# A two-layer transformer tower on one core: the out-projection moved to the end of its slot, its residual and norm to the next slot, and the transposes of h1 ahead of the embedding

## The chip, the core and the metric

The kernel runs on one core of a Trainium2 chip. Its engines each take their own instructions in program order: TensorE (PE, with its weight loads shown apart as PEld), VectorE (DVE), ScalarE (ACT), GpSimd (POOL) and SyncE (SP, which here only issues DMAs). They wait for each other through semaphores. The metric is the device time of one execution in microseconds. Every kernel is timed in several runs, and one execution is also profiled.

## What is computed

64 images of 3 x 112 x 112 are cut into 49 patches of 16 x 16 each, which makes 3136 tokens of 192 values. Then, with every value in float32:

```
h   = patches @ W.T                                  # embedding, 768 -> 192
h1  = layernorm(h  + attention1(h))                  # 12 heads of 16, causal, with relative positions
out = layernorm(h1 + attention2(h1))                 # qkv = h1 @ Wqkv.T + bqkv + delta
# delta: softmax router over 8 experts, the best 2 kept, a low-rank product of rank 16 each
# attention2 has no mask; layernorm(x) = (x - mean) / sqrt(var + 1e-5), without scale or shift
```

Attention works inside one image of 49 tokens. Both attentions end in an out-projection, a matmul of the attended values (192) with a 192 x 192 matrix and a bias.

## The kernel before

The work has two grains. **Tiles** are 2 images, 98 tokens (32 of them); attention proper works on tiles. **Blocks** are 128 tokens (25 of them, b = 0 to 24, the last with 64); every product over tokens works on blocks. A tile and a layer together make one **slot**: slots 0 to 7 are layer 1 of tiles 0 to 7, then layers 2 and 1 alternate (even slots layer 2, odd slots layer 1) until layer 1 is done in slot 55; slots 56 to 63 are layer 2. Each engine has its own list, written as one loop over the slots n, and runs it in order. The lists are the same on each run, and no planner moves instructions beyond what follows.

In slot n PE computes the scores of that slot's tile (L466 adds the causal mask in layer 1, L472 is q times k). It transposes the probabilities of the slot before (L497) and weights the values with them (L508). DVE takes the row maxima of the scores (L763), subtracts them (L770), waits for ACT's exponential (L653), sums (L775), inverts (L780) and scales (L784). That last step releases L497 of the next slot. ACT copies PSUM to SBUF: the transposed probabilities `pt` (L667), the weighted values `yt` (L672).

The products over blocks are spread over the slots. For a block b, in this order of slots:

- `embed` (L414, 6 steps, each matmul issued as two) writes bank 5, ACT's `take_h` (L627) copies it to h.
- `turns`: `transpose_h` (L426, L427, bank 6), then q, k, v of layer 1 (`project_v` L484 in bank 6, `project_qk1` L436 and L438 in bank 4). ACT's `take_qk` copies k (L644) and then q (L646) out of bank 4 and raises `qk_ready`.
- `out1`: two slots after its last tile, `out_project` (L519, L520) writes bank 5. DVE adds the residual (`add_residual`, L791) and takes the statistics (`ln_stats` L797, `ln_aggregate` L803). ACT takes a logarithm and an exponential (`inverse_deviation`, L699 and L702). POOL computes a shift (L385) and h1 = res * rstd + shift (L388).
- `turns1`: the slot after `out1`. `transpose_h1` (L530) writes bank 4, ACT's `take_h1` (L680) copies it, and at the end of the same slot `route` (L540, L542) computes the router's input in bank 7.
- `routers`: the slot after that, DVE's `router_max` and `combine` (L808 to L829), then PE's `transpose_hw` (L548, L549).
- `qkv2s`: `project_v` (L484) and `project_qk2` (L449, L451, L453, bank 4) for layer 2.
- `out2`: as `out1` for layer 2, and SP stores the block.

EMBED, QKV1 and QKV2, the tables that say which slot a block's products fall into, come from a small balancing loop at the head of the file; it is the same in both kernels.

Two variables carry PSUM's bank rules: `bank4` and `bank5` hold the semaphore that the next user of the bank must wait for. After `project_qk` the next user of bank 4 waits for `qk_ready`; after `transpose_h1` it waits for `h1t_ready`. After `embed` the next user of bank 5 waits for `h_ready`; after `out_project`, for `res_ready`. `transpose_probs` waits for `yt_ready` of the weighting before it, since both use bank 2.

Below are the functions that the change touches.

Of the kernel before, what the change touches and what calls it, by code (L numbers as in the profile page):

```python
# [71 lines left out]
SLOT1 = [CHAINS.index((1, t)) for t in range(TILES)]  # L72
# [10 lines left out]
DONE1 = [SLOT1[last_tile(b)] + (b == BLOCKS - 1) for b in range(BLOCKS)]  # L83
DONE2 = [SLOT2[last_tile(b)] + (b == BLOCKS - 1) for b in range(BLOCKS)]
FIRST = -3
SLOTS = max(DONE2) + 3


WORK = {n: 0.0 for n in range(-9, SLOTS)}
# [82 lines left out]
def build(nc, x, tok_w, w1a_in, w1b_in, pos_in, const_in, p1_in, lora_in, w2_in, b2_in, p2_in, out):  # L172
    with ExitStack() as ctx:
# [132 lines left out]
        @block.sync  # L306
        def _(sp):
            def load_x(b):
                sp.dma_start(xs[:, b % XS], x[b]).then_inc(x_loaded[b % XS], 16)

            for u in range(3):
                sp.dma_start(xs[:, 0, 2 * u:2 * u + 2], x[0, :, 2 * u:2 * u + 2]).then_inc(x0_loaded[u], 16)
            load_x(1)
            sp.dma_start(w1a[:], w1a_in).then_inc(w1a_loaded, 16)
            sp.dma_start(w1b[:], w1b_in).then_inc(w1b_loaded, 16)
            sp.dma_start(tail[64:128, 0:POS], pos_in[:, 0:POS]).then_inc(pos_loaded[0], 16)
            load_x(2)
            load_x(3)
            sp.dma_start(p1[:], p1_in).then_inc(p1_loaded, 16)
            sp.dma_start(tail[64:128, POS:TOK], pos_in[:, POS:TOK]).then_inc(pos_loaded[1], 16)  # L320
            sp.dma_start(lora[:], lora_in).then_inc(lora_loaded, 16)
            load_x(4)
            sp.dma_start(w2[:], w2_in).then_inc(w2_loaded, 16)
            sp.dma_start(b2[:], b2_in).then_inc(b2_loaded, 16)
            sp.dma_start(p2[:], p2_in).then_inc(p2_loaded, 16)

            def place_values(L, t, slot_of):
                sp.wait_ge(L.v_rows, block_of(t) + 1)
                if t >= VB:
                    sp.wait_ge(pv_done, slot_of[t - VB] + 1)  # L330
                for b, row, s, at, k in moves(t):
                    for e in range(2):
                        sp.dma_start(L.vbd[t % VB][e * PB + at:e * PB + at + k, s].rearrange("p (u e c) -> p u e c", u=3, e=2)[:, :, e],
                                     L.vrow[b % VR][row:row + k, e * C:(e + 1) * C].rearrange("p (u c) -> p u c", u=3)).then_inc(L.v_ready[t % VB], 16)

            sp.wait_ge(zeros_ready, 2)
            for n in range(FIRST, SLOTS):
                for b in embeds(n):
                    if b + XS < BLOCKS:
                        sp.wait_ge(emb_done, b + 1)  # L340
                        load_x(b + XS)
                for t in tiles_from(n - 1, QKV1):
                    place_values(L1, t, SLOT1)
                for t in tiles_from(n - 1, QKV2):
                    place_values(L2, t, SLOT2)
                for b in out2(n):
                    k = tokens(b)
                    sp.wait_ge(L2.ln_ready, b + 1)
                    sp.dma_start(out[first_token(b):first_token(b) + k], o_sb[b % OS][0:k]
                                 ).then_inc(out_stored[b % OS], 16)  # L350
            for u in range(OS):
                sp.wait_ge(out_stored[u], 16 * len(range(u, BLOCKS, OS)))

        @block.gpsimd
        def _(pool):
# [35 lines left out]
            block_diagonal(0)  # L391
            block_diagonal(1)
            for n in range(SLOTS):
                for b in out1(n):
                    normalise(L1, b, h[0:tokens(b), b, :])
                for b in out2(n):
                    if b >= OS:
                        pool.wait_ge(out_stored[b % OS], 16 * (b // OS))
                    normalise(L2, b, o_sb[b % OS][0:tokens(b)])
                block_diagonal(n + 2)  # L400

        @block.tensor
        def _(pe):
# [158 lines left out]

            for n in range(FIRST, SLOTS):
                layer, t = attention(n)
                before, u = attention(n - 1)
                if layer == 1:
                    scores(L1, t, n)
                if layer == 2:
                    scores(L2, t, n)
                for b in out1(n):  # L570
                    if b == 0:
                        pe.wait_ge(p1_loaded, 16)
                        pe.wait_ge(ones_ready, 1)
                    bank5 = out_project(L1, p1, b, SLOT1, bank5)
                for b in out2(n):
                    if b == 0:
                        pe.wait_ge(p2_loaded, 16)
                    bank5 = out_project(L2, p2, b, SLOT2, bank5)
                for b in turns(n):
                    bank6 = transpose_h(b, bank6)  # L580
                if before:
                    if n == 1:
                        pe.wait_ge(zeros_ready, 2)
                    transpose_probs(n - 1)
                for b in turns1(n):
                    bank4 = transpose_h1(b, bank4)
                for b in qkv2s(n):
                    pe.wait_ge(hwt_ready, b + 1)
                    if b == 0:
                        pe.wait_ge(w2_loaded, 16)  # L590
                        pe.wait_ge(b2_loaded, 16)
                    bank6 = project_v(L2, b, values2(b), bank6)
                    bank4 = project_qk2(b, bank4)
                for b in turns(n):
                    pe.wait_ge(ht_ready, b + 1)
                    if b == 0:
                        pe.wait_ge(w1a_loaded, 16)
                        pe.wait_ge(w1b_loaded, 16)
                        pe.wait_ge(pos_loaded[0], 16)
                    if first_token(b) + tokens(b) > POS >= first_token(b):  # L600
                        pe.wait_ge(pos_loaded[1], 16)
                    bank6 = project_v(L1, b, values1(b), bank6)
                    bank4 = project_qk1(b, bank4)
                for b in embeds(n):
                    bank5 = embed(b, bank5)
                if before == 1:
                    weigh_values(L1, u, n - 1)
                if before == 2:
                    weigh_values(L2, u, n - 1)
                for b in routers(n):  # L610
                    transpose_hw(b)
                for b in turns1(n):
                    if b == 0:
                        pe.wait_ge(lora_loaded, 16)
                    route(b)

        @block.scalar
        def _(act):
# [85 lines left out]

            for n in range(FIRST, SLOTS):
                layer, t = attention(n)
                before, u = attention(n - 1)
                for b in routers(n):
                    router_exp(b)
                for b in turns(n):  # L710
                    take_ht(b)
                if before:
                    take_pt(n - 1)
                for b in turns1(n):
                    take_h1(b)
                if n == 0:
                    act.wait_ge(masks_ready, 1)
                if layer:
                    exponent(n)
                for b in qkv2s(n):  # L720
                    take_v(L2, b, SLOT2)
                    take_qk(L2, b, SLOT2)
                for b in out1(n):
                    inverse_deviation(L1, b)
                for b in out2(n):
                    inverse_deviation(L2, b)
                for b in turns(n):
                    take_v(L1, b, SLOT1)
                    take_qk(L1, b, SLOT1)
                for b in embeds(n):  # L730
                    take_h(b)
                if before:
                    take_y(n - 1, u)
                for b in routers(n):
                    take_hw(b)

        @block.vector
        def _(dve):
# [94 lines left out]

            for n in range(SLOTS):
                layer, t = attention(n)
                for b in routers(n):
                    router_max(b)
                if layer:
                    largest(n)
                    subtract(n)  # L840
                for b in out1(n):
                    add_residual(L1, b)
                for b in out2(n):
                    add_residual(L2, b)
                for b in out1(n):
                    ln_stats(L1, b)
                for b in out2(n):
                    ln_stats(L2, b)
                for b in routers(n):
                    combine(b)  # L850
                for b in out1(n):
                    ln_aggregate(L1, b)
                for b in out2(n):
                    ln_aggregate(L2, b)
                if layer:
                    sum_probs(n)
                    invert_sums(n)
# [80 lines left out]
```

## Time and profile before

| what | value |
|---|---|
| median of 3 runs | 447.51 us (447.36 to 451.51) |
| the profiled execution, whole | 446.53 us |
| its span, first to last instruction | 444.7 us |
| mean granted clock of TensorE | 0.958 of full |
| PE, PEld, DVE, ACT, POOL busy | 398.6, 348.5, 295.0, 231.7, 116.6 us |

The profiled execution is 0.98 us below the median. The span lacks 1.8 us that lie around it. In the profile a row of the timeline gives the start in microseconds from the span's start, the busy time, the engine, the source line, the operation, what it writes and reads, and in brackets how long the engine stood idle before it and for whom it waited. Ends of matmuls are modelled and overlap the start of the next, so PE's pace is read from start to start.

The slots can be told apart in the timeline by the start of L472. Slot 13 begins at 119.35, slot 14 at 124.83, slot 15 at 129.24, slot 24 at 185.10 and slot 25 at 192.56.

### The profile page before, as it was taken

How to read it: one execution, taken by the hardware profiler on the slowest of the kernel's cores; microseconds unless marked ns; L12 is line 12 of the kernel's file. 1: busy time of each engine (PE TensorE's matmuls, PEld its weight loads, DVE VectorE, ACT ScalarE, POOL GpSimd, SP SyncE). 2: the span in 40 equal slices, each digit the busy share in tenths (PEclk: the TensorE clock that was granted, in tenths of full speed). 3: DMA queues.
4: the chain of work that ended last, by engine and by line, in shares of the span. 5: the costliest groups of instructions: out<-in, count | busy, mean ns of one | idle time of the engine just before them, and what ended most of it. 6: DMA issues, size and time to landing. Idle time of an engine off the chain costs nothing.

```text
span 444.7 us, 13552 instructions
## 1 busy us (share of the span) xinstructions
PE 398.6 (90%) x5270; PEld 348.5 (78%) x5270; DVE 295.0 (66%) x783; ACT 231.7 (52%) x727; POOL 116.6 (26%) x237
## 2 busy tenths in 40 slices
PE   5874997999989999999999999989998999887974
PEld 4763886878878898889888899778886988776853
DVE  7051566857677676876687767696578758777572
ACT  1341455465565656555665555646655565544442
POOL 1110112230233213432242222333223223313122
PEclk9995999999999999999999999999999999996875
DMA  8452221210212111220221212111101110111010
GB/s 282 131 159 63 50 80 18 51 38 15 48 28 62 50 48 28 64 54 11 50 64 25 57 45 58 28 19 30 18 19 19 30 18 19 17 23 22 14 32 23
DMA packets 49353, 21.23 MB, mean 48 GB/s; under 512 B 41278, under 2 KB 45601, under 8 KB 49226
## 3 DMA queue, kind: packets, MB, share of 16 engines
q1 hardware_dynamic: 48714, 19.64, 18.1%
q8 instruction: 42, 0.69, 0.6%
q10 hardware_dynamic: 576, 0.73, 0.5%
q14 instruction: 21, 0.17, 0.1%
HBM read 13.13 MB, written 2.41 MB: 35 GB/s over the span
## 4 chain that ended last, share of the span: by engine, by line
PE 73%; ACT 9%; DVE 8%; issue 5%; DMA 3%; SPq 1%; POOLq 0%; POOL 0%; ACTq 0%; DVEq 0%
PE ps L414 11%; PE ps L484 10%; PE ps L497 8%; PE ps L472 7%; PE ps L519 5%; PE ps L508 5%; PE ps L449 4%; PE ps L453 4%; PE ps L451 4%; PE ps L436 3%; PE ps L438 3%; PE ps L520 3%; DVE mx L763 2%; PE ps L540 2%; ACT q L646 2%
## 5 line engine op out<-in xcount | busy, mean ns | idle before, releaser
L763 DVE TENSOR_REDUCE mx<-ps 113x12 f32<-113x588 f32 x64 | 49.2, 769 | 75.4 <-PE ps L472 74.8
L378 POOL TENSOR_SCALAR kbd<-k,const 64x294 f32<-64x294 f32 x128 | 69.1, 549 | 98.1 <-ACT q L646 88.0
L667 ACT COPY pt<-ps 113x339 f32<-113x339 f32 x128 | 50.7, 445 | 52.1 <-PE ps L497 51.7
L385 POOL TENSOR_SCALAR shift<-mv,rstd 128x1 f32<-128x1 f32 (+1 forms) x50 | 13.2, 264 | 216.4 <-ACT rstd L702 216.4
L414 PE MATMUL ps<-tokw,xs 128*128 128x192 f32 (+1 forms) x300 | 57.1, 342 | 9.1 <-DVE res L791 4.8
L775 DVE TENSOR_REDUCE psum<-probs 113x12 f32<-113x588 f32 x64 | 48.4, 756 | 23.7 <-ACT probs L653 22.9
L414 PEld LDWEIGHTS ps<-tokw,xs 128*128 128x128 f32 (+1 forms) x300 | 50.7, 197 | 11.4 <-DVE res L791 6.4
L497 PE MATMUL ps<-const,probs 113*113 113x113 f32 x384 | 52.1, 274 | 3.4 <-DVE probs L784 2.6
L784 DVE TENSOR_TENSOR probs<-probs,rsum 113x588 f32<-113x588 f32 x64 | 51.4, 802 | 2.2
L497 PEld LDWEIGHTS ps<-const,probs 113*113 113x113 f32 x384 | 47.2, 186 | 6.6 <-issue 5.1
L770 DVE TENSOR_TENSOR probs<-ps,mx 113x588 f32<-113x588 f32 x64 | 49.4, 772 | 2.2
L644 ACT COPY k<-ps 64x384 f32<-64x384 f32 (+11 forms) x60 | 24.0, 417 | 51.4 <-PE ps L453 40.6
L472 PE MATMUL ps<-kbd,q 32*49 32x98 f32 x1536 | 47.5, 252 | 0.0
L653 ACT ACTIVATE probs<-probs 113x588 f32<-113x588 f32 x64 | 45.6, 713 | 2.4 <-DVE probs L770 1.2
L508 PE MATMUL ps<-pt,vbd 113*32 113x49 f32 x1536 | 36.8, 214 | 10.9 <-DMA vbd<-vrow 9.6
L508 PEld LDWEIGHTS ps<-pt,vbd 113*32 113x32 f32 x1536 | 27.9, 112 | 21.7 <-DMA vbd<-vrow 9.8
L472 PEld LDWEIGHTS ps<-kbd,q 32*49 32x49 f32 x1536 | 34.0, 120 | 9.0 <-issue 3.8
L519 PE MATMUL ps<-p,yt 96*128 96x192 f32 (+1 forms) x100 | 30.7, 390 | 8.3 <-ACT yt L672 6.7
L449 PE MATMUL ps<-h1t,w 96*128 96x128 f32 (+1 forms) x150 | 29.4, 277 | 0.0
L436 PE MATMUL ps<-ht,w1a 128*128 128x128 f32 (+1 forms) x150 | 29.3, 276 | 0.0
L451 PE MATMUL ps<-h1t,w 105*128 105x128 f32 (+1 forms) x150 | 29.2, 276 | 0.0
L453 PE MATMUL ps<-hwt,b 128*128 128x128 f32 (+1 forms) x150 | 29.2, 276 | 0.0
(79 smaller groups left out, 704.2 us busy)
## 6 DMA issues: line engine op xcount, KB each, us to landing
xs<-in_x SPq DMA_DIRECT2D x24, 384.0 KB, 3.7
vbd<-vrow SPq DMA_DIRECT2D x160, 18.4 KB
out<-o SPq DMA_DIRECT2D x24, 96.0 KB, 1.7
tail<-in_pos SPq DMA_DIRECT2D x1, 656.0 KB, 16.2
tokw<-in_tokw ACTq DMA_DIRECT2D x3, 192.0 KB, 3.4
w<-in_w SPq DMA_DIRECT2D x1, 472.5 KB, 10.0
xs<-in_x SPq DMA_DIRECT2D x3, 128.0 KB, 3.2
p<-in_p SPq DMA_DIRECT2D x2, 145.5 KB
```

Source lines behind the costliest of these rows:

```text
L378: last = nc.gpsimd.tensor_scalar(L.kbd[t % 2][:, e], L.k[:, :, at:at + T], kmask[:, e:e + 1], 1.0, ALU.mult, ALU.mult)
L414: last = nc.tensor.matmul(ps[0:k, 5, 0:E], xs[:, b % XS, m, 0:k], tokw[:, m, :], start=(m == 0), stop=(m == KX - 1))
L449: nc.tensor.matmul(ps[:, 4, m * NB:m * NB + k], w2[0:C, 1, cols], h1t[0:C, 1, b % HB2, 0:k], start=True, stop=False)
L472: last = nc.tensor.matmul(ps[s * PB:s * PB + S, half, m * T:(m + 1) * T], L.q[32 * half:32 * half + 32, m, at + s * S:at + (s + 1) * S], L ...
L497: last = nc.tensor.transpose(ps[0:PP, 2 + half, g * PP:(g + 1) * PP], pf[:, k:k + PP], ident[0:PP, 0:PP])
L508: last = nc.tensor.matmul(ps[32 * g:32 * g + 32, 2, half * T + s * S:half * T + (s + 1) * S], values[:, s, (3 * half + g) // 2, :, (3 * ha ...
L519: nc.tensor.matmul(ps[0:k, 5, 0:E], yt[0:C, 1, lo:lo + k], w[0:C, 1, :], start=True, stop=False)
L667: nc.scalar.copy(pt[n % 2][:, 3 * half:3 * half + 3, :].rearrange("p g i -> p (g i)"), ps[0:PP, 2 + half, 0:3 * PP]).then_inc(pt_ready[hal ...
L763: nc.vector.tensor_reduce(mx[:].rearrange("p (b h) -> p b h", b=2), score_view, AX.X, ALU.max).then_inc(mx_ready, 1)
L770: nc.vector.tensor_tensor(probs_view(n), score_view, spread(mx), ALU.subtract).then_inc(sub_ready, 1)
L775: nc.vector.tensor_reduce(psum[:].rearrange("p (b h) -> p b h", b=2), probs_view(n), AX.X, ALU.add).then_inc(sum_ready, 1)
L784: nc.vector.tensor_tensor(probs_view(n), probs_view(n), spread(rsum), ALU.mult).then_inc(p_ready, 1)
```

## The change

PE's list within a slot was: scores, out-projection, transposes of h, transposes of the probabilities, transposes of h1, q, k, v of layer 2, q, k, v of layer 1, embedding, weighting, the router's parts. It is now: scores, transposes of h, transposes of the probabilities, q, k, v of layer 2 and of layer 1, transposes of h1, embedding, out-projection, weighting, the router's parts. On DVE the residual, the statistics and the aggregate stand at the head of the next slot's list, ahead of the router's maximum and the row maxima. On ACT `inverse_deviation` stands in the next slot between `take_ht` and `take_pt`, and `take_h1` follows the copies of q and k. On POOL the normalisation, and on SP the store of a block, are one slot later. The loops run over one slot more, so that the last block's norm is reached.

```diff
--- before.py
+++ after.py
@@ -83,7 +83,7 @@
 DONE1 = [SLOT1[last_tile(b)] + (b == BLOCKS - 1) for b in range(BLOCKS)]
 DONE2 = [SLOT2[last_tile(b)] + (b == BLOCKS - 1) for b in range(BLOCKS)]
 FIRST = -3
-SLOTS = max(DONE2) + 3
+SLOTS = max(DONE2) + 4
 
 
 WORK = {n: 0.0 for n in range(-9, SLOTS)}
@@ -343,7 +343,7 @@
                     place_values(L1, t, SLOT1)
                 for t in tiles_from(n - 1, QKV2):
                     place_values(L2, t, SLOT2)
-                for b in out2(n):
+                for b in out2(n - 1):
                     k = tokens(b)
                     sp.wait_ge(L2.ln_ready, b + 1)
                     sp.dma_start(out[first_token(b):first_token(b) + k], o_sb[b % OS][0:k]
@@ -391,9 +391,9 @@
             block_diagonal(0)
             block_diagonal(1)
             for n in range(SLOTS):
-                for b in out1(n):
+                for b in out1(n - 1):
                     normalise(L1, b, h[0:tokens(b), b, :])
-                for b in out2(n):
+                for b in out2(n - 1):
                     if b >= OS:
                         pool.wait_ge(out_stored[b % OS], 16 * (b // OS))
                     normalise(L2, b, o_sb[b % OS][0:tokens(b)])
@@ -567,23 +567,12 @@
                     scores(L1, t, n)
                 if layer == 2:
                     scores(L2, t, n)
-                for b in out1(n):
-                    if b == 0:
-                        pe.wait_ge(p1_loaded, 16)
-                        pe.wait_ge(ones_ready, 1)
-                    bank5 = out_project(L1, p1, b, SLOT1, bank5)
-                for b in out2(n):
-                    if b == 0:
-                        pe.wait_ge(p2_loaded, 16)
-                    bank5 = out_project(L2, p2, b, SLOT2, bank5)
                 for b in turns(n):
                     bank6 = transpose_h(b, bank6)
                 if before:
                     if n == 1:
                         pe.wait_ge(zeros_ready, 2)
                     transpose_probs(n - 1)
-                for b in turns1(n):
-                    bank4 = transpose_h1(b, bank4)
                 for b in qkv2s(n):
                     pe.wait_ge(hwt_ready, b + 1)
                     if b == 0:
@@ -601,8 +590,19 @@
                         pe.wait_ge(pos_loaded[1], 16)
                     bank6 = project_v(L1, b, values1(b), bank6)
                     bank4 = project_qk1(b, bank4)
+                for b in turns1(n):
+                    bank4 = transpose_h1(b, bank4)
                 for b in embeds(n):
                     bank5 = embed(b, bank5)
+                for b in out1(n):
+                    if b == 0:
+                        pe.wait_ge(p1_loaded, 16)
+                        pe.wait_ge(ones_ready, 1)
+                    bank5 = out_project(L1, p1, b, SLOT1, bank5)
+                for b in out2(n):
+                    if b == 0:
+                        pe.wait_ge(p2_loaded, 16)
+                    bank5 = out_project(L2, p2, b, SLOT2, bank5)
                 if before == 1:
                     weigh_values(L1, u, n - 1)
                 if before == 2:
@@ -709,10 +709,12 @@
                     router_exp(b)
                 for b in turns(n):
                     take_ht(b)
+                for b in out1(n - 1):
+                    inverse_deviation(L1, b)
+                for b in out2(n - 1):
+                    inverse_deviation(L2, b)
                 if before:
                     take_pt(n - 1)
-                for b in turns1(n):
-                    take_h1(b)
                 if n == 0:
                     act.wait_ge(masks_ready, 1)
                 if layer:
@@ -720,13 +722,11 @@
                 for b in qkv2s(n):
                     take_v(L2, b, SLOT2)
                     take_qk(L2, b, SLOT2)
-                for b in out1(n):
-                    inverse_deviation(L1, b)
-                for b in out2(n):
-                    inverse_deviation(L2, b)
                 for b in turns(n):
                     take_v(L1, b, SLOT1)
                     take_qk(L1, b, SLOT1)
+                for b in turns1(n):
+                    take_h1(b)
                 for b in embeds(n):
                     take_h(b)
                 if before:
@@ -833,25 +833,25 @@
 
             for n in range(SLOTS):
                 layer, t = attention(n)
+                for b in out1(n - 1):
+                    add_residual(L1, b)
+                for b in out2(n - 1):
+                    add_residual(L2, b)
+                for b in out1(n - 1):
+                    ln_stats(L1, b)
+                for b in out2(n - 1):
+                    ln_stats(L2, b)
+                for b in out1(n - 1):
+                    ln_aggregate(L1, b)
+                for b in out2(n - 1):
+                    ln_aggregate(L2, b)
                 for b in routers(n):
                     router_max(b)
                 if layer:
                     largest(n)
                     subtract(n)
-                for b in out1(n):
-                    add_residual(L1, b)
-                for b in out2(n):
-                    add_residual(L2, b)
-                for b in out1(n):
-                    ln_stats(L1, b)
-                for b in out2(n):
-                    ln_stats(L2, b)
                 for b in routers(n):
                     combine(b)
-                for b in out1(n):
-                    ln_aggregate(L1, b)
-                for b in out2(n):
-                    ln_aggregate(L2, b)
                 if layer:
                     sum_probs(n)
                     invert_sums(n)
```

**PE, slot 14** (layer 2 of tile 3, no product of q, k, v in it; `yt_ready` is ACT's copy of the weighted values, `ln_ready1` POOL's norm of layer 1). Before:

```order
L472 MATMUL ps<-kbd_1,q 49x98 x11
L519 MATMUL ps<-p,yt 128x192 [waits yt_ready,res_ready1]
L520 MATMUL ps<-p,yt 128x192
L497 MATMUL ps<-const,probs 113x113 [waits p_ready,yt_ready]
L497 MATMUL ps<-const,probs 113x113 x5
L530 MATMUL ps<-const,h 96x128 [waits ln_ready1,qk_ready1]
L530 MATMUL ps<-const,h 96x128
L508 MATMUL ps<-pt,vbd_2 32x49 [waits pt_ready0,v_ready1_2]
```

and now:

```order
L472 MATMUL ps<-kbd_1,q 49x98 x11
L497 MATMUL ps<-const,probs 113x113 [waits p_ready,yt_ready]
L497 MATMUL ps<-const,probs 113x113 x5
L530 MATMUL ps<-const,h 96x128 [waits ln_ready1,qk_ready1]
L530 MATMUL ps<-const,h 96x128
L519 MATMUL ps<-p,yt 128x192 [waits yt_ready,res_ready1]
L520 MATMUL ps<-p,yt 128x192
L508 MATMUL ps<-pt,vbd_2 32x49 [waits pt_ready0,v_ready1_2]
```

The out-projection went from ahead of the transposes to directly ahead of the weighting, and the norm that `ln_ready1` stands for now starts with DVE's residual in this slot, not in the one before.

**PE, slot 16** (layer 2 of tile 4, with the q, k, v of a block; `qk_ready2` is ACT's copy of q and k out of bank 4, `h1t_ready` its copy of the transposed h1 out of the same bank). Before:

```order
L530 MATMUL ps<-const,h 96x128 [waits ln_ready1,h1t_ready]
L530 MATMUL ps<-const,h 96x128
L484 MATMUL ps<-w,h1t 128x192 [waits v_rows1,hwt_ready]
L484 MATMUL ps<-w,h1t 128x192
L484 MATMUL ps<-b,hwt 128x192
L449 MATMUL ps<-h1t,w 128x128 [waits h1t_ready]
```

and now:

```order
L449 MATMUL ps<-h1t,w 128x128
L451 MATMUL ps<-h1t,w 128x128
L453 MATMUL ps<-hwt,b 128x128
L530 MATMUL ps<-const,h 96x128 [waits ln_ready1,qk_ready2]
L530 MATMUL ps<-const,h 96x128
L519 MATMUL ps<-p,yt 128x192 [waits yt_ready,res_ready1]
```

The two users of bank 4 changed places: three matmuls of another bank (L484) stood between them, and now none does.

**PE, slot 15** (layer 1 of tile 11, with an embedding). Before:

```order
L519 MATMUL ps<-p,yt 128x192 [waits yt_ready,res_ready2]
L520 MATMUL ps<-p,yt 128x192
L497 MATMUL ps<-const,probs 113x113 [waits p_ready,yt_ready]
L497 MATMUL ps<-const,probs 113x113 x5
L414 MATMUL ps<-tokw,xs 128x192 [waits x_loaded0,res_ready1]
L414 MATMUL ps<-tokw,xs 128x192 x5
```

and now:

```order
L497 MATMUL ps<-const,probs 113x113 [waits p_ready,yt_ready]
L497 MATMUL ps<-const,probs 113x113 x5
L414 MATMUL ps<-tokw,xs 128x192 [waits x_loaded0,res_ready2]
L414 MATMUL ps<-tokw,xs 128x192 x5
L519 MATMUL ps<-p,yt 128x192 [waits yt_ready,h_ready]
L520 MATMUL ps<-p,yt 128x192
```

The two users of bank 5 changed places too: the embedding waited for DVE's residual, and now the out-projection waits for ACT's copy of h.

## Rows read from the trace of the kernel before

**Rows 1.** The page: span, busy time, and the chain that ended last.
```profile
span 444.7 us, 13552 instructions
PE 398.6 (90%) x5270; PEld 348.5 (78%) x5270; DVE 295.0 (66%) x783; ACT 231.7 (52%) x727; POOL 116.6 (26%) x237
...
PE 73%; ACT 9%; DVE 8%; issue 5%; DMA 3%; SPq 1%; POOLq 0%; POOL 0%; ACTq 0%; DVEq 0%
```

**Rows 2.** Waits: engine, line, releaser: us in total, times, longest.
```profile
PE ps L519 <- ACT yt L672: 6.7, 16, 0.7
...
PE ps L414 <- DVE res L791: 4.8, 7, 0.9
...
PE ps L540 <- ACT hwt L694: 4.8, 5, 1.5
...
PE ps L508 <- ACT pt L667: 1.0, 5, 0.4
```

**Rows 3.** Timeline, all engines, end of slot 24.
```profile
190.87 0.39 PE L453 MATMUL ps<-hwt,b 128*128 128x128 f32 x2
...
191.19 0.55 PE L508 MATMUL ps<-pt,vbd 113*32 113x49 f32 x24
191.30 0.47 ACT L644 COPY k<-ps 64x384 f32<-64x384 f32 x1 [1.61 <-PE ps L453]
...
191.67 0.50 PE L540 MATMUL ps<-lora,h1t 96*128 96x136 f32 x2
191.78 0.48 ACT L646 ACTIVATE q<-ps 64x384 f32<-64x384 f32 x1
```

**Rows 4.** Timeline, head of slot 24.
```profile
186.11 0.31 ACT L672 COPY yt<-ps 96x196 f32<-96x196 f32 x1
...
186.57 0.56 PE L519 MATMUL ps<-p,yt 96*128 96x192 f32 x2 [0.74 <-ACT yt L672]
...
187.29 0.76 PE L497 MATMUL ps<-const,probs 113*113 113x113 f32 x6
```

**Rows 5.** Timeline of PE, before slot 0: an embedding, then transposes of its h.
```profile
12.35 2.12 PE L414 MATMUL ps<-tokw,xs 128*128 128x192 f32 x12
14.96 0.30 PE L426 MATMUL ps<-const,h 128*128 128x128 f32 x1 [0.50 <-ACT h L627]
```

**Rows 6.** Timelines of DVE, ACT and POOL, slot 31: residual to norm.
```profile
230.87 0.35 DVE L791 TENSOR_TENSOR res<-ps,h 128x192 f32<-128x192 f32 x1
...
231.65 0.18 DVE L803 BATCH_NORM_AGGREGATE mv<-st 128x2 f32<-128x6 f32 x1
...
232.36 0.20 ACT L702 ACTIVATE rstd<-lnv 128x1 f32<-128x1 f32 x1
...
233.02 0.50 POOL L388 TENSOR_SCALAR h<-res,rstd,shift 128x192 f32<-128x192 f32 x1
```

**Rows 7.** Timelines of DVE (first row) and PE, slot 14 and the start of 15.
```profile
124.46 0.89 DVE L784 TENSOR_TENSOR probs<-probs,rsum 113x588 f32<-113x588 f32 x1
...
124.83 0.72 PE L472 MATMUL ps<-kbd,q 32*49 32x98 f32 x24
...
126.63 0.76 PE L497 MATMUL ps<-const,probs 113*113 113x113 f32 x6
127.22 0.38 PE L530 MATMUL ps<-const,h 128*96 128x128 f32 x2
...
129.24 0.72 PE L472 MATMUL ps<-kbd,q 32*49 32x98 f32 x24
```

**Rows 8.** Windows: stretch, its length, busy us of each engine, granted clock, DMA.
```profile
66.00:69.60 3.60, 2.41 (x39) 1.98 (x38) 2.87 (x12) 2.69 (x9) 1.52 (x3) 1.00 0.15 23
...
400.50:404.00 3.50, 2.11 (x52) 1.53 (x43) 2.90 (x10) 2.73 (x11) 3.07 (x8) 1.00 0.10 31
404.00:414.00 10.00, 8.60 (x52) 7.59 (x53) 7.84 (x24) 2.68 (x8) 0.38 (x1) 0.51 0.10 16
...
424.50:428.00 3.50, 2.00 (x55) 1.56 (x53) 2.85 (x8) 1.97 (x6) 1.64 (x4) 1.00 0.16 43
```

## The prediction

> **What bounds the kernel now.** I read the page first, for who is busy: PE 398.6 us of the 444.7 us span, no other engine over 66%, and 73% of the chain that ended last lies on PE [rows 1]. The list of waits then says what PE still waits for: in the body of the program only short things, 6.7 us in 16 waits for `yt` ahead of the out-projection, 4.8 us in 7 waits of the embedding for the residual, 4.8 us in 5 waits of `route` for `hwt`, 1.0 us for `pt` [rows 2]. So PE's list runs nearly without a gap, and the other engines have slack. The third view is the timeline, slot by slot. It gives PE's pace from start to start, and for the change it gives the one thing that matters: how long after PE's last write into a bank the copy out of it is done. A wait that is taken from PE's list is a gain at most as large as these rows, a wait that is put into it is a loss in full, as nothing stands behind PE that could make it up.
>
> **The change, part by part.** It removes no instruction and adds none; every term is a wait on PE that goes or comes. The counts come from the lists of both kernels.
>
> *Transposes of h1 directly after q and k (bank 4).* In 19 slots (4, 5, 6, 8, 9, 10, 16, 18, 24, 26, 28, 32, 34, 36, 42, 44, 50, 52, 58) L530 now follows the last matmul of q and k and must wait until ACT has copied k and then q out of bank 4. In slot 24 the last L453 pair starts at 190.87, the copies begin at 191.30 and end at 192.26, and PE went on with L508 at 191.19 [rows 3]. A copy's end reaches PE 0.15 later: `yt` ends at 186.42, L519 starts at 186.57 [rows 4]. So L530 would start at 192.41 where PE could have gone on at about 191.16: 1.25 us each, **+23.8**. It was hidden before because the order was the other way round: ACT's one copy of h1 was covered by the value matmuls.
>
> *Out-projection directly after the embedding (bank 5).* In 16 slots (3, 4, 7, 9, 15, 17, 22, 25, 27, 30, 33, 35, 41, 43, 49, 51) it waits for `take_h`. The same pair, an embedding and something that needs its copy, stands before slot 0: L414 from 12.35 for 2.12, and the next PE instruction at 14.96, with 0.50 of shown idle and 0.56 against PE's pace [rows 5]. **+9.0**.
>
> *Transposes of h1 in slots without q, k, v.* In slots 14, 22, 40, 48, 56 and 59 nothing stands between the transposes of the probabilities and L530, and the norm now starts with the residual at this slot's head. From the residual's start to the norm's end took 2.65 us in slot 31 (230.87 to 233.52) [rows 6]. PE reaches L530 1.24 after the slot's start: 0.65 for the scores and 0.59 from L497 to L530 [rows 7]. When does the residual start? DVE must first finish the probabilities of the slot before, which it did 0.52 into slot 14 (125.35 against 124.83) [rows 7]. The transposes of the probabilities in slot 13 come 1.1 earlier (0.72 of out-projection [rows 4] and its share of the `yt` waits, 0.4, no longer stand ahead), ACT's logarithm and exponential, now ahead of `pt`, take back 0.5, and the slot itself is 0.4 shorter: 0.3 into the slot. So L530 waits 0.3 + 2.65 - 1.24 = 1.7, of which I take 1.6, as ACT's queue will be shorter than in slot 31, for slots 14, 22, 40 and 48. Slots 56 and 59 follow long slots, in which the residual starts right behind the out-projection, 0.25 before the slot's end: 1.2 each. **+8.8**.
>
> *Behind that.* `route` needs the copy of h1. In the 7 of the 19 slots without an out-projection only the weighting (0.48, L508 to L540 [rows 3]) lies between L530 and `route`; transposing, copying and telling PE take about 0.2 more: **+1.4**. At the end of the program the out-projection of block 22 moves from a gap in PE to between the last transposes and the last weighting: 0.72 of issue, at half clock **+1.4**.
>
> *What goes.* The embedding finds bank 5 free: **-4.8** [rows 2]. The `yt` waits come from ACT being busy with q and k when the weighting ends; the out-projection now stands between them (0.72 longer) and the longest of them was 0.74: **-6.7** [rows 2]. The `pt` waits are covered: **-1.0**. ACT has copied q and k by the time `route` waits for `hwt`, so of 4.8 some **-1.5** goes.
>
> DVE: the residual, statistics and aggregate (0.96 from 230.87 to 231.83 [rows 6]) move from the shadow of the exponential to the slot's head, where DVE otherwise waits for the scores. It costs PE nothing as long as slots are long, which they now are; if that cover is gone the row maxima come late and the next transposes with them, up to 0.4 in some short slots, which I leave to the range. POOL gets its norm earlier in a slot, and its `kbd` work is for two slots later; SP's store stands behind the value DMAs, which have slots to spare. Both: nothing.
>
> Sum: 23.8 + 9.0 + 8.8 + 1.4 + 1.4 - 4.8 - 6.7 - 1.0 - 1.5 = **+30.4**. Against the profiled execution's 446.53 us that is 476.9; the median of the runs is 0.98 higher, so 478.
>
> *The clock.* TensorE's granted clock went from 1.00 to about half (2.4 to 1.2 GHz) at 404, after a stretch of 3.50 us in which PE was busy 2.11, and again after 424.5 to 428.0 with 2.00 of 3.50. It did not after 66.0 to 69.6 with 2.41 of 3.60 [rows 8]. The new waits of 1.6 us in slots 14, 22, 40 and 48, between work of small tiles, make stretches like the first two. One dip costs what PE does in 10 us at half clock: 8.60 busy would have been 4.3 [rows 8], less what its own waits would have taken there, 3.7. I cannot tell whether a given wait sets it off, and bound it by none (0) and by all six short slots (+22). I take one more than before: **+3.7**, nearer the low end, as the new stretches are no emptier than the two that fell and stand among full ones. Forecast: **482**.
>
> **Rivals.**
>
> *The clock falls often.* All six short slots, and some of the 19, whose wait of 1.25 is followed by the weighting and a short wait of `route`, bring the clock down. For it: PE was busy 60% before the clock fell at 404, and the new stretches come near that. Against it: slot 5's wait of 1.5 [rows 2] lies in the stretch that brought no fall. Six dips: 478 + 22 = 500.
>
> *The waits are smaller.* The norm is ready in the short slots (DVE earlier, ACT's queue free), no dip is added, and ACT's copies overlap PE's modelled end more than I read: q and k at 1.0, h at 0.45. 19 x 1.0 + 16 x 0.45 + 3 + 1 - 14 = +16: 463. For it: ends of matmuls are modelled. Against it: the 0.15 is a measured gap.
>
> *Not slower.* The new waits are made up, because PE's list is not what sets the pace: its weight loads fill only 348.5 us [rows 1], and 96 us of the span have none. If PE issues tighter after each wait, only the removed waits count: 446.5 - 14 + 1 = 433.5, or up to 450 with part of it. It decides if the matmuls after a wait start closer together than those without; but L508 follows L453 at the pace of the others, and L519 to L497 took 0.72 behind a wait of 0.74 [rows 4], the pace of work without one, so I hold it unlikely. The Trainium skill (Perfetto Trace Analysis, section Identifying the Most-Contended Engine) says that the matmul busy share is not a good measure of how near a kernel is to its limit and that the share of weight loads is; by it this kernel would have a fifth of its span to give. The same page (Optimizing Tensor Performance, Matmuls) asks that independent groups rotate through banks so that a copy overlaps the next group's matmuls, which the new order gives up in banks 4 and 5; by it the sum stands.
>
> That the change does not do what it says can be left out: the lists show the moves.
>
> **The numbers.** The forecast of 482 (own range 474 to 491) has 0.47, the clock 0.25, smaller waits 0.24, not slower 0.04. The range reaches halfway into both neighbours, 464 to 500, and leaves out less than 2 in 10. A change under 1% could not be told from none: faster by more than that 0.02 and within it 0.02, both from the last rival; slower 0.96.
>
> **What would show it.** In the waits of the changed kernel: L530 for ACT's q, 19 times and near 1.15 us shown; L519 for ACT's h, 16 times near 0.5; L530 for POOL's h, about 6 times, over 1 us; `yt` and residual waits of L519 and L414 nearly gone. PE's idle grows by about 30 us and its busy time only with the clock. The prediction is wrong if L530's waits for q are few or short, or if the time grows far beyond PE's idle at full clock.

## The result, and the profile after

The changed kernel takes 477.62 us (median of 4 runs, 473.4 to 481.71), the kernel before beside it 449.51 us (447.36 to 452.06): ratio 1.059, 95% interval 1.048 to 1.071. The profiled execution took 476.86 us with a span of 475.1 us, 30.4 us more than the span before. The median lies inside the range of 464 to 500 and 4.4 us under the forecast of 482; slower was the forecast. Ratios and intervals, here and below, leave out runs that took over 1.5% longer than the fastest of their kernel.

The page after, against [rows 1]: PE was busy 9 us longer, and idle some 21 us longer. The new waits are shown some 0.2 us shorter than they hold PE up (1.06 against 1.27 below), as they are counted from the modelled end of the matmul before them; that part counts as busy here, beside what the clock costs.

```profile
span 475.1 us, 13552 instructions
PE 407.7 (86%) x5270; PEld 349.3 (74%) x5270; DVE 297.3 (63%) x783; ACT 240.5 (51%) x727; POOL 110.8 (23%) x237
```

The list of waits after, against [rows 2] (us in total, times, longest):

```profile
PE ps L530 <- ACT q L646: 20.6, 19, 1.2
...
PE ps L519 <- ACT h L627: 6.7, 16, 0.6
PE ps L530 <- POOL h L388: 6.2, 6, 1.2
...
PE ps L540 <- ACT hwt L694: 3.3, 5, 0.7
...
PE ps L508 <- ACT pt L667: 1.0, 1, 1.0
...
PE ps L519 <- ACT yt L672: 0.5, 1, 0.5
```

The first three lines are new, with the counts 19, 16 and 6 that the lists of instructions gave. The 16 waits for `yt` are down to one, and the waits of the embedding for the residual are gone.

The end of slot 24 after, all engines, against [rows 3]:

```profile
206.82 0.39 PE L453 MATMUL ps<-hwt,b 128*128 128x128 f32 x2
...
207.25 0.48 ACT L644 COPY k<-ps 64x384 f32<-64x384 f32 x1 [0.97 <-PE ps L453]
207.73 0.48 ACT L646 ACTIVATE q<-ps 64x384 f32<-64x384 f32 x1
...
208.27 0.42 PE L530 MATMUL ps<-const,h 128*96 128x128 f32 x2 [1.06 <-ACT q L646]
```

PE used to start its next work 0.32 us after the start of the last L453 pair; now 1.45 us pass. The shown idle, 1.06, is counted from the modelled end of the matmul.

Slot 27 after (PE; an embedding and the next to need its copy out of the bank, as in [rows 5], now in the body):

```profile
227.34 2.12 PE L414 MATMUL ps<-tokw,xs 128*128 128x192 f32 x12
229.87 0.59 PE L519 MATMUL ps<-p,yt 96*128 96x192 f32 x2 [0.41 <-ACT h L627]
```

Slot 14 after, first DVE's residual, then POOL's norm and PE, against [rows 6, 7]:

```profile
133.99 0.35 DVE L791 TENSOR_TENSOR res<-ps,h 128x192 f32<-128x192 f32 x1
```
```profile
135.99 0.50 POOL L388 TENSOR_SCALAR h<-res,rstd,shift 128x192 f32<-128x192 f32 x1
...
136.63 0.40 PE L530 MATMUL ps<-const,h 128*96 128x128 f32 x2 [1.20 <-POOL h L388]
```

From the residual to the norm's end 2.50 us pass, and 0.14 more until PE starts. The slot began at 133.93.

Windows after (length, busy us of PE, PEld, DVE, ACT, POOL, then the granted clock). The first is slot 15, the second slot 49 with the same work, the third slot 19, the fourth slot 45 with the same work:

```profile
140.21:147.57 7.36, 6.95 (x75) 5.95 (x73) 5.20 (x16) 2.69 (x9) 1.74 (x4) 0.73 0.17 33
365.49:371.01 5.52, 5.11 (x74) 4.23 (x72) 5.20 (x20) 2.63 (x9) 1.79 (x4) 1.00 0.13 21
170.97:178.94 7.97, 7.97 (x88) 7.24 (x86) 4.59 (x15) 4.05 (x12) 1.00 (x2) 0.79 0.06 10
343.05:349.65 6.60, 6.59 (x88) 5.85 (x86) 4.59 (x15) 3.87 (x12) 1.43 (x2) 1.00 0.08 12
```

The clock fell twice in the body, once behind slot 14's wait for the norm and once behind slot 18, whose wait for q and k is followed by the weighting and `route`. Slot 15 is 1.8 us and slot 19 1.4 us longer than its like. Slot 14 itself took 6.28 against 5.05 of slot 40, which carries the same work. The fall does not follow from the wait alone: slots 40 and 48 of this execution have the same wait of 1.19 for the norm, and the granted clock stayed at 1.00 behind it.

### The profile page after: what moved, and what is told of

The parts are those of the page before. It is cut to its first block, busy times and chain, and to the rows that moved or that the text cites. A ratio compares the mean times of both kernels' runs of the same rounds, so it can differ in the third digit from the quotient of the medians.

```text
span 475.1 us, 13552 instructions
## 1 busy us (share of the span) xinstructions
PE 407.7 (86%) x5270; PEld 349.3 (74%) x5270; DVE 297.3 (63%) x783; ACT 240.5 (51%) x727; POOL 110.8 (23%) x237
## 4 chain that ended last, share of the span: by engine, by line
PE 73%; ACT 8%; SPq 7%; DVE 6%; issue 4%; DMA 1%; POOL 1%; POOLq 0%
PE ps L414 9%; PE ps L484 8%; PE ps L497 8%; PE ps L472 8%; PE ps L508 6%; PE ps L519 4%; SPq L309 4%; PE ps L449 4%; PE ps L453 4%; PE ps L451 4%; PE ps L520 3%; PE ps L540 2%; PE ps L436 2%; PE ps L438 2%; PE ps L530 2%
## 5 line engine op out<-in xcount | busy, mean ns | idle before, releaser
L378 POOL TENSOR_SCALAR kbd<-k,const 64x294 f32<-64x294 f32 x128 | 70.9, 564 | 203.9 <-ACT q L646 195.5
L497 PE MATMUL ps<-const,probs 113*113 113x113 f32 x384 | 55.3, 283 | 4.7 <-DVE probs L784 4.7
L414 PEld LDWEIGHTS ps<-tokw,xs 128*128 128x128 f32 (+1 forms) x300 | 52.2, 202 | 4.5 <-DMA xs<-in_x 4.1
L497 PEld LDWEIGHTS ps<-const,probs 113*113 113x113 f32 x384 | 45.9, 188 | 11.1 <-issue 5.8
L784 DVE TENSOR_TENSOR probs<-probs,rsum 113x588 f32<-113x588 f32 x64 | 49.5, 773 | 2.2
L385 POOL TENSOR_SCALAR shift<-mv,rstd 128x1 f32<-128x1 f32 (+1 forms) x50 | 13.4, 267 | 145.9 <-ACT rstd L702 145.9
L791 DVE TENSOR_TENSOR res<-ps,h 128x192 f32<-128x192 f32 (+1 forms) x50 | 17.8, 355 | 45.7 <-PE ps L520 45.7
L672 ACT COPY yt<-ps 96x196 f32<-96x196 f32 x64 | 20.3, 318 | 51.3 <-PE ps L508 50.0
L519 PE MATMUL ps<-p,yt 96*128 96x192 f32 (+1 forms) x100 | 27.6, 359 | 8.1 <-ACT h L627 6.7
L530 PE MATMUL ps<-const,h 128*96 128x128 f32 (+1 forms) x50 | 10.3, 288 | 26.8 <-ACT q L646 20.6
```

The source lines that it names most:

```text
L378: last = nc.gpsimd.tensor_scalar(L.kbd[t % 2][:, e], L.k[:, :, at:at + T], kmask[:, e:e + 1], 1.0, ALU.mult, ALU.mult)
L414: last = nc.tensor.matmul(ps[0:k, 5, 0:E], xs[:, b % XS, m, 0:k], tokw[:, m, :], start=(m == 0), stop=(m == KX - 1))
L497: last = nc.tensor.transpose(ps[0:PP, 2 + half, g * PP:(g + 1) * PP], pf[:, k:k + PP], ident[0:PP, 0:PP])
L519: nc.tensor.matmul(ps[0:k, 5, 0:E], yt[0:C, 1, lo:lo + k], w[0:C, 1, :], start=True, stop=False)
L784: nc.vector.tensor_tensor(probs_view(n), probs_view(n), spread(rsum), ALU.mult).then_inc(p_ready, 1)
```

## The experiments

All times are medians of all runs, with the kernel before run beside them on the same chip. The runs come from several chips, on which the kernel before took 449.2 (the h1 move, h1 in bank 6, the out-projection in bank 4, h1 early again), 449.5 (the h1 move filled, both banks, the out-projection first) and 446.8 us (both banks filled, the changed kernel filled). So up to 2.7 us of a difference between two of these groups lie between the chips. Theory: PE waits for the copies out of bank 4 and bank 5 and for the norm, and these waits, with the half-clock stretches they bring, are the loss. Rivals: the late norm alone is the loss; or PE would have waited at the same places for something else; or the clock only follows from the time and costs nothing itself.

### The h1 move alone, on the kernel before

On PE (on ACT `take_h1` goes behind the copies of q and k in the same way):

```diff
-                for b in turns1(n):
-                    bank4 = transpose_h1(b, bank4)
                 for b in qkv2s(n):
 ...
                 for b in turns(n):
 ...
+                for b in turns1(n):
+                    bank4 = transpose_h1(b, bank4)
                 for b in embeds(n):
```

> The kernel before, with one part of the change alone: the transposes of h1 (L530) stand behind the q and k products on PE, and their copy behind the copies of q and k on ACT. Out-projection, residual and norm stay where they were. Theory (bank 4: L530 waits 1.25 us for the copies of k and q in 19 slots): +23.8 us, less the `yt` and `hwt` waits that the longer slot covers (2 to 4), so 467 to 472 against 447.5; the waits show L530 for ACT's q 19 times at 1.06. Rival (the loss of the whole change comes from the late norm, and L530's wait is covered once the norm is early): within 1% of before. Rival (the parts only cost together): under +10.

Measured: 488.2 us (481.8 to 494.3) against 449.2: 39 us more by the medians, 33 and 35 for the two runs at a granted clock of 0.932. Either is beyond what was expected (467 to 472), and more than the whole change costs. The waits for q are there as expected; one wait was not expected, that of `route` for the copy of h1:

```profile
PE ps L530 <- ACT q L646: 22.1, 19, 1.8
...
PE ps L540 <- ACT h1t L680: 4.2, 5, 1.0
```

It comes from ACT's order: `take_h1` stands behind `inverse_deviation`, which waits for DVE. Waits of this size do not make 38 us, by which the profiled span (482.7 us, clock 0.932) is longer than before. The windows of the body (before, then this kernel) show the rest:

```profile
50.00:400.00 350.00, 332.89 (x4580) 293.25 (x4579) 250.02 (x683) 200.17 (x633) 99.80 (x194) 1.00 0.16 36
```
```profile
50.00:440.00 390.00, 351.08 (x4578) 307.18 (x4577) 250.52 (x683) 206.70 (x639) 99.80 (x197) 0.96 0.15 33
```

The same matmuls kept PE busy 18 us longer, at a granted clock of 0.96. By an estimate from that mean some 31 us of the 390 were at half clock (2 x 0.04 x 390). The runs agree with it: spans of 480.0 and 482.7 us came with a clock of 0.932, 490.1 with 0.914 and 492.5 with 0.910.

### The same, with the waits filled

```diff
+                if turns1(n) and (qkv2s(n) or turns(n)):
+                    pe.wait_ge(*bank6)
+                    for _ in range(4):
+                        nc.tensor.matmul(ps[:, 6, 256:384], ident, ident, start=True, stop=True)
                 for b in turns1(n):
                     bank4 = transpose_h1(b, bank4)
```

> The before kernel with the h1 move alone, and four unused 128-column matmuls into bank 6 in each of the 19 slots, in the 1.25 us in which L530 waits for ACT. They leave out nothing and change no result. Theory (the move alone costs 39 us, because besides some 26 us of waits TensorE's clock is granted at half for about 28 us more than before, which costs about half of that): PE does more work, the half-clock stretches in the body of the program mostly go, granted clock back to 0.95 or above, and the time falls to 470 to 476 from 488. Rival (the clock is a consequence and not a cause): 486 or more, by the added work if it does not fit in the waits.

Measured: 474.7 us (474.0 to 475.8), ratio to before 1.057 (1.049 to 1.065). PE does more and the kernel is 13.4 us faster than without it by the medians, 8.4 us against its two runs at 0.932, and each of its runs is faster than each run of the h1 move alone. The clock in the body is back at 1.00:

```profile
50.00:430.00 380.00, 356.35 (x4747) 312.59 (x4750) 251.15 (x686) 207.31 (x642) 101.30 (x198) 1.00 0.15 34
```

So the clock is a cause, and the rival that it only follows from the time is refuted. What the move costs without the falls in the body is the 25.2 us that remain by the medians (474.7 against 449.5), 27.5 by the profiled spans. The four matmuls do not lengthen the wait: slot 36 takes 8.07 with them and without. But the 25.2 are not bank 4's wait alone, for which 19 x 1.25 = 23.8 was forecast: `route`'s new wait of 4.2 is in them, less some of the waits for `hwt` and the residual.

### h1 in bank 6

```diff
-                    last = nc.tensor.transpose(ps[0:C, 4, c * NB:c * NB + k], ...
+                    last = nc.tensor.transpose(ps[0:C, 6, c * NB:c * NB + k], ...
...
-                    bank4 = transpose_h1(b, bank4)
+                    bank6 = transpose_h1(b, bank6)
     # ACT: take_v, take_h1 (which reads bank 6), then take_qk; in the changed kernel take_h1 comes last
```

> The changed kernel, but the transposes of h1 go to bank 6, whose last user is the value product that ACT has copied long before, and ACT copies h1 ahead of q and k. Theory (bank 4's wait is the largest term): L530's 19 waits for ACT's q vanish, 1.23 us each, so 477 - 23 = 453 to 456; the waits for the norm in six slots stay near 1.2, those for h near 0.41. Rival (ACT or the norm would have held PE up at the same place anyway): less than 8 us gained, the wait shown on another releaser, such as POOL's h in many slots, or `yt`.

Measured: 451.5 us (449.1 to 456.6), ratio to before 1.007 (1.003 to 1.011): 26 us less than the change, and a little under the 453 to 456 that were expected. In the profiled executions the 19 slots are together 22.9 us shorter than in the changed kernel, 1.27 in most, and slots 14, 15 and 19 are 4.4 us shorter, as the clock stayed at 1.00 there. PE at the same place as above, now without a wait, as the value product's copy out of bank 6 has long ended:

```profile
193.34 0.39 PE L453 MATMUL ps<-hwt,b 128*128 128x128 f32 x2
193.56 0.38 PE L530 MATMUL ps<-const,h 128*96 128x128 f32 x2
```

In the list of waits L530 waits only for POOL's h, 6 times, as in the changed kernel. Little took the place of bank 4's wait: in slots 6 and 10 `route` now waits 1.42 for `hwt` instead of 0.67, so that they gained 0.5 only. That refutes the rival that PE would have waited there anyway, and the one that the late norm is the loss. Slot 14 waits 1.18 for the norm, as in the changed kernel, and here no fall of the clock follows.

### The out-projection in bank 4 where there is an embedding

```diff
+                    if embeds(n):
+                        bank4 = out_project(L1, p1, b, SLOT1, bank4, 4)
+                    else:
+                        bank5 = out_project(L1, p1, b, SLOT1, bank5, 5)
     # the same for layer 2; add_residual reads the bank that was written
```

> The changed kernel, but in the 16 slots with an embedding the out-projection writes bank 4, which ACT has copied during the embedding, and DVE adds the residual from there. In the other slots it stays in bank 5. Theory (bank 5's wait costs 0.56 us in 16 slots): -9, so 468. Rival (the wait is shown at 0.41 but the weighting behind it would have waited for `pt` or `yt` anyway): less than 3 us gained.

Measured: 467.3 us (465.2 to 473.1), ratio 1.038 (1.032 to 1.045): 10.3 less than the change, for 16 x 0.56 = 9.0 expected. The waits of L519 for h are gone from its list; L530's are what they were (20.6 in 19). As a check on one slot, slot 35 took 7.31 before, 7.93 with the change and 7.25 here.

### h1 transposed early again

On PE (ACT's `take_h1` goes back behind `take_pt`):

```diff
+                for b in turns1(n):
+                    bank4 = transpose_h1(b, bank4)
                 for b in qkv2s(n):
 ...
-                for b in turns1(n):
-                    bank4 = transpose_h1(b, bank4)
                 for b in embeds(n):
```

> The changed kernel with one part undone: the transposes of h1 and their copy stand where they were before, behind the transposes of the probabilities and ahead of q, k and v. Theory: bank 4 no longer makes L530 wait, but the norm, which now starts at the slot's head, does: its end lies 1.8 to 3.0 us into the 19 slots, and PE is there after 1.24 to 1.46, so waits of 0.7 to 1.6 us, 24 us in all take the place of the 23 that go: 473 to 481, L530 waiting 25 times for POOL's h. Rival (only bank 4 costs): 454.

Measured: 479.0 us (476.9 to 480.8), ratio 1.066 (1.058 to 1.074): no better than the change, as the theory expected. One wait has taken the other's place:

```profile
PE ps L530 <- POOL h L388: 27.0, 25, 1.6
```

So once the residual stands at the next slot's head, neither of the two places tried is good for h1's transposes in bank 4: early they wait for the norm, late for q and k.

### Both banks, then the out-projection first, then the waits filled

The first takes the two edits of the banks together.

> The changed kernel with both new waits taken away: h1 transposed into bank 6 (copied ahead of q and k), and the out-projection in bank 4 in slots with an embedding. Theory (the two bank waits are nearly the whole loss and do not overlap): 451.5 less the 10 that bank 5's wait cost = 441 to 443, which is faster than before by what the change took away in `yt`, `pt` and residual waits. Rival (without them another wait, for the probabilities or the norm, takes their place): 446 to 451.

Measured: 445.7 us (438.6 to 449.8), ratio 0.981 (0.971 to 0.991). The ratio stands on three of the six runs, at clocks of 0.945 to 0.960, which took 438.6 to 442.9 us; the other three, at 0.930 to 0.934, took 448.6 to 449.8 and so were no faster than the median of the kernel before, 449.5. At the higher clock the kernel is faster than before by some 2%; over all six runs the medians differ by 3.8 us, less than the runs of either kernel spread. The median is 3 us above what was expected. The rival's new wait did appear, but small: L497 for the probabilities, 6.8 us in 10 waits, 4.7 in 4 with the change.

The second puts the out-projection ahead of h1's transposes in slots without an embedding.

> As the kernel with both waits taken away, and in slots without an embedding the out-projection stands ahead of the transposes of h1, where in five slots (14, 40, 48, 56 and partly none in 59) PE waits for the norm. Theory: 0.76 us of it is covered in four slots, -3, so 438 to 440. Rival: no difference, as the weighting then waits for `pt`.

Measured: 443.3 us (440.9 to 449.2), ratio 0.984 (0.977 to 0.991). That can't be told from the kernel without it, and the expected 438 to 440 did not come. The wait of L530 for h fell from 6.2 to 3.7 us, that of L497 for the probabilities rose from 6.8 to 8.1. In the profiled executions slots 14, 40 and 48 are 0.53 us shorter each, as the theory had it, but slots 16, 42 and 50 are 0.4 to 0.5 longer, and from slot 13 to slot 55 it takes 251.6 us against 250.6: what is won in one slot is lost in another.

The third adds to the first:

```diff
     # ahead of h1's transposes in slots without q, k, v, and ahead of route where it waits for hwt
+                        pe.wait_ge(*bank6)
+                        for _ in range(4):
+                            nc.tensor.matmul(ps[:, 6, 256:384], ident, ident, start=True, stop=True)
```

> As the kernel with both bank waits taken away, and four unused 128-column matmuls into bank 6 where PE still waits over 1 us: ahead of the transposes of h1 in slots 14, 22, 40, 48, 56, 59, and ahead of the router's product in slots 5, 6, 9, 10, 59. Theory (its runs spread from 438.6 to 449.8 with the granted clock, from 0.96 to 0.93, and the waits are what brings the clock down): the runs draw together near 439 to 442 and the clock stays at 0.95 or above. Rival (the clock falls for what stands at the start and end, which is not filled): the same spread, 440 to 450.

Measured: 435.9 us (433.2 to 436.9), ratio 0.976 (0.973 to 0.979), the fastest kernel here and below the expected 439 to 442. Its median is 9.8 us under that of the kernel without the unused matmuls, but 2.7 of that lie between the chips, and most of the rest is that the clock was 0.960 to 0.971 in all six runs, while it was 0.930 to 0.945 in four runs of the other. By the ratios the two differ by 0.5%, within their intervals. What the filling is shown to do here is to draw the runs together, from a spread of 11.1 us to 3.7, near the faster ones; the rival, the same spread, is refuted.

### The changed kernel, filled

The same four matmuls ahead of h1's transposes in all 25 slots of the changed kernel.

> The changed kernel, with four unused 128-column matmuls into bank 6 ahead of the transposes of h1 in all 25 slots, where PE waits 1.06 to 1.2 us for the copies or the norm. Theory (of the 28 us that the change costs some 4 to 5 are half-clock stretches in the body): 471 to 474, clock 0.955 or above. Rival (the added work delays PE more than the clock gives back): 478 or more.

Measured: 468.7 us (467.6 to 468.7), ratio 1.049 (1.047 to 1.051): 8.9 less than the change, of which 2.7 lie between the chips; by the ratios it is 1%, or 4.6 us of the kernel before. In the profiled executions slots 14, 15 and 19 are together 4.4 us shorter, as expected, and what is left lies at the start and the end. The body's clock is 1.00 and the runs agree within 1.2 us, while those of the change spread over 8.

Separate columns of bank 4 for the two users, without the wait, would be another way. The Trainium skill (PSUM — Partial Sum Buffer, section PSUM bank collisions raise a hardware error) says that two engines collide when they use one bank in the same 32 partitions at once, even at different addresses in it. No run here shows it; it was not tried.

## Why the prediction was right

The direction, the mechanism and the counts held. The sizes, step by step, are read in the profiled executions from start to start:

- **Bank 4, +23.8.** 19 waits, 1.06 us shown in most. Slot 36, which changed in nothing else that costs time, went from 6.68 to 7.95, 1.27 longer. Against the kernel with h1 in bank 6 the 19 slots are 22.9 us longer.
- **Bank 5, +9.0.** 16 waits; slot 27 went from 7.31 to 7.93, 0.62 each, so 9.9. Taking the wait away gave 10.3.
- **The norm in short slots, +8.8.** Six waits. In slots 14, 22, 40 and 48 the transposes of h1 started 2.04 after those of the probabilities, against 0.59, so 1.45 each against 1.6; in slots 56 and 59 it was 1.0 and 0.8 against 1.2. That makes 7.6: the residual started 0.06 us into slot 14, not 0.3, and the norm came 2.50 after it, not 2.65. No run takes all of this term away alone.
- **`route` behind the copy of h1, +1.4.** Too large: in slots 18, 26, 34, 44 and 52 the product starts 0.61 to 0.62 after the weighting, not 0.48, which makes 0.7. In the other two of the seven, 6 and 10, it waits for `hwt` anyway.
- **What goes, -14.** The waits for `yt` went from 6.7 to 0.5, those of the embedding from 4.8 to none, `hwt` from 4.8 to 3.3. The `pt` waits went in the body, and one of 1.0 came at the end. As a shown wait is shorter than what it costs, more went than was added up from the list: from slot 3 to slot 59 the time grew by 24.0 us apart from the clock, and beside the terms above that leaves some 17 for what went.
- **The end, +1.4.** From slot 60's start to the end it took 37.6 us before and 37.9 after: +0.2. Three waits for `yt` went there, which the term before has too, and those for the probabilities grew from 1.7 to 4.1.
- **DVE's move at nothing.** Right in the body: L497 waited 0.4 in slot 30 and 0.2 in slot 54. Whether it has a part in the longer waits for the probabilities at the end is open.
- **The clock, +3.7.** In the profiled execution slots 14, 15 and 19 are together 4.4 us longer than their likes at full clock: the size was right. The places were so in part. One fall came behind a short slot, as forecast, the other behind slot 18, one of the 19.

The profiled spans differ by 30.4 us, the very number of the sum without its clock term. That the two agree is luck: +4.4 of clock in the body and +1.8 at the start (slot 2 begins 0.87 later and is 0.89 longer, at half clock) stand against a norm, a `route` and an end that were too large and a gain that was too small. By the medians the change cost 28.1 us beside the kernel before, where 34 were forecast. Two of the signs named were off as well: the waits for q show 1.06, not near 1.15, and PE's idle grew by 21 us, not 30.

Of the rivals, smaller waits at 463 had 1.0, 0.45 and 3 us for the three terms, and they came at 1.27 in most of the 19 slots, 0.62 and 7.6; the 0.15 us from a copy's end to PE showed again as 0.14 after the norm. The clock falling often, at 500, did not come for the change, but the h1 move alone has a body at 0.96. *Not slower* failed: behind the wait in slot 24 the next matmuls start 0.26 and 0.33 us apart, and 0.22 and 0.32 in the kernel without that wait, so nothing was made up. The weight loads' share of 78% that spoke for it fell to 74%, and the room that it seemed to leave was not there.

## What to carry to other kernels

On an engine whose list has no gaps, look at each pair of neighbours in one PSUM bank: if the second follows the first directly, the copy's time (here 0.96 us for two copies, or 0.32 for one, and 0.3 around it) is paid in full, and another bank whose last user is long done removes it. Before moving a consumer later to dodge one wait, look at what its producer's new place and its new neighbour will make it wait for. And ask of short waits on TensorE whether they cost a second time through the clock: here 19 waits did so in one kernel and hardly in another, so it has to be read from the granted clock of several runs. A few unused matmuls in a wait that can't be removed can pay.

## What the runs showed of the hardware

The granted clock of TensorE fell from full to half behind single waits of 1.06 us (slot 18) and 1.20 us (slot 14 of the changed kernel), and not each time: behind the same wait for the norm as in slot 14, 1.19, it did not fall in its slots 40 and 48, nor in slot 14 of the kernel with h1 in bank 6. It differs from run to run. The h1 move alone ran with 0.932 down to 0.910 on the same code, in spans of 480.0 to 492.5 us; the same kernel with 76 unused matmuls in its waits held 0.953 to 0.961 and stayed within 1.8 us. By an estimate from these means, for each microsecond more at half clock the span grew by about half a microsecond: 0.932 over 480.0 is 65 us at half clock, 0.910 over 492.5 is 89 us, some 23 us more for 12.5 us of span.
